# Attention's end in a four-layer graph network: one quad summed per stage of the last softmax, and the last scores ahead of the small TensorE steps

## The reference, cut to what matters

```python
q = x @ Wq + bq; k = x @ Wk + bk; v = x @ Wv + bv; skip = x @ Ws + bs
logits = jnp.sum(q[dst] * k[src], axis=-1) * (1.0 / jnp.sqrt(d))
m = segment_max(logits, dst); e = jnp.exp(logits - m[dst]); z = segment_sum(e, dst)
alpha = e / jnp.maximum(z[dst], 1e-16)
x = segment_sum(alpha[:, None] * v[src], dst) + skip       # relu after layers 1 and 2
```

## Time and profile before

| | us |
|---|---|
| three executions | 7211.72, 7203.6, 7215.84 |
| median | 7211.72 |
| span of the profiled execution | 7212.5 |
| ends of the three attention layers, from small step 0 of piece 13 to the last add | 41.29, 39.97, 37.98 |

### The profile page before, as it was taken

How to read it: one execution, slowest core, us unless ns; L and a number is a source line. 1 busy time by engine, 2 the same in 40 slices (tenths; PEclk the granted TensorE clock), 3 DMA queues, 4 the chain that set the end, 5 groups by cost and what they waited for, 6 DMA issues and landing times. The chain is left out here.

```text
span 7212.5 us, 119527 instructions
## 1 busy us (share of the span) xinstructions
PE 5515.6 (76%) x30306; PEld 4153.5 (58%) x30345; DVE 4706.7 (65%) x20339; ACT 2265.8 (31%) x5973; POOL 4972.2 (69%) x5179
## 2 busy tenths in 40 slices
PE   5675667776777766777777776789899997889887
PEld 4442344555666555566656665666666665667665
DVE  7985668466666446666636666664544546888887
ACT  1044442211114311113421111543333333554454
POOL 5777765677777477777577777647576574777774
PEclk6687888788888878888878888889999998988898
DMA  9433352577777467767557777657566773222222
GB/s 306 135 79 88 78 114 52 155 204 207 206 208 218 149 186 210 208 203 216 175 165 210 208 208 206 204 164 211 166 208 188 210 208 93 56 57 56 56 57 54
DMA packets 911842, 1151.30 MB, mean 160 GB/s; under 512 B 143281, under 2 KB 676465, under 8 KB 911249
## 3 DMA queue, kind: packets, MB, share of 16 engines
q1 hardware_dynamic: 689440, 673.54, 30.9%
q0 software_dynamic: 202464, 461.07, 23.9%
q10 hardware_dynamic: 19346, 9.66, 0.5%
HBM read 882.09 MB, written 261.74 MB: 159 GB/s over the span
## 5 line engine op out<-in xcount | busy, mean ns | idle before, releaser
L500 POOL DMA_INDIRECT G<-table_kv,idx x2496 | 2383.7, 955 | 966.5 <-issue 753.8
L1710 DVE SCALAR_TENSOR_TENSOR sums<-ramp,place,bank 128x128 f32<-128x128 f32 x2496 | 717.4, 342 | 1192.0 <-PE bank L1629 1098.4
L1619 PE MATMUL bank<-ident,G 128*128 128x128 f32 x2496 | 637.9, 334 | 720.1 <-DMA G<-table_kv,idx 713.5
L2144 POOL DMA_INDIRECT G<-table_h,src_idx x864 | 828.4, 959 | 465.0 <-issue 252.0
L1598 ACT COPY slab<-bank 128x512 f32<-128x512 f32 x624 | 364.8, 585 | 2295.3 <-PE bank L1619 2294.6
L500 POOL DMA_INDIRECT G<-table_h,idx x832 | 826.3, 993 | 298.2 <-issue 226.7
L1629 PE MATMUL bank<-qT,slab 128*128 x4992 | 915.5, 341 | 100.3 <-issue 80.4
L1629 PEld LDWEIGHTS bank<-qT,slab 128*128 128x128 f32 x4992 | 803.1, 244 | 196.0 <-issue 195.2
L1619 PEld LDWEIGHTS bank<-ident,G 128*128 128x128 f32 x2496 | 377.6, 163 | 931.2 <-DMA G<-table_kv,idx 891.7
L1841 DVE TENSOR_SCALAR OH<-ramp,place,weight 128x128 f32<-128x128 f32 x2076 | 715.4, 354 | 15.6 <-issue 8.5
L2128 PE MATMUL bank<-sums,qT 128*128 128x418 bf16 (+1 forms) x3528 | 676.4, 334 | 38.7 <-DVE same L2051 13.9
(11 more groups left out here) (355 smaller groups left out, 9538.6 us busy)
## 6 DMA issues: line engine op xcount, KB each, us to landing
stash<-G SPq DMA_DIRECT2D x312, 512.0 KB
sums<-stash SPq DMA_DIRECT2D x624, 256.0 KB
sums<-adjacency SPq DMA_DIRECT2D x294, 522.5 KB
adjacency<-same SPq DMA_DIRECT2D x49, 1184.0 KB, 13.9
same<-adjacency SPq DMA_DIRECT2D x90, 522.5 KB
G<-table_kv,idx POOLq DMA_INDIRECT x2496
sums<-adjacency SPq DMA_DIRECT2D x48, 408.0 KB
table_kv<-G SPq DMA_DIRECT2D x72, 256.0 KB, 3.2
```

The costliest lines, as they stand in the source:

```text
L500: pool.indirect_dma_start(G[:, s, 0:width], None, tab, bass.IndirectOffsetOnAxis(ap=idx[:, s:s + 1], axis=0)).then_inc(c_gather[s].sem, 16)
L1619: ins = pe.transpose(bank[q % 2][:, (s % QUAD) * P:(s % QUAD + 1) * P], G[:, s, 0:D], ident[:])
L1710: ins = dve.scalar_tensor_tensor(scratch[:, s, :], ramp[:], place[:, n * QUAD + s:n * QUAD + s + 1], bank[2 + q % 2][:, s * P:(s + 1) * P] ...
L2144: pool.indirect_dma_start(G[:, s, 0:D], None, table[l], bass.IndirectOffsetOnAxis(ap=src_idx[:, DENSE + t:DENSE + t + 1], axis=0)).then_in ...
```

## The change

```diff
@@ sums_by_slot
-                most = 1 if n < HASTE else 2
+                most = 1 if n < HASTE or ALL_QUADS <= n < weights_slot(PIECES - 1) else 2
                 found[n] = []
                 while len(found[n]) < most and q < ALL_QUADS and weights_slot(piece_of(q)) + (piece_of(q) >= HASTY_PIECE) <= n:
+                    if found[n] and q == LAST:
+                        break
                     found[n].append(q)
...
-        RESCALED = {c: weights_slot(c) if c >= HASTY_PIECE else SUM_SLOT[first_quad(c)] for c in range(PIECES)}
+        RESCALED = {c: max(weights_slot(c), SUM_SLOT[first_quad(c) - 1]) if c >= HASTY_PIECE else SUM_SLOT[first_quad(c)] for c in range(PIECES)}
+        FIRST_ONEHOTS = {c: max(weights_slot(c), SUM_SLOT[first_quad(c) - 2]) for c in range(HASTY_PIECE, PIECES)}
@@ first_onehots
-            return [first_quad(c) + k for c in (0, *range(HASTY_PIECE, PIECES)) if (weights_slot(c) if c else LAG_QUADS) == n for k in range(2)]
+            return [first_quad(c) + k for c in (0, *range(HASTY_PIECE, PIECES)) if (FIRST_ONEHOTS[c] if c else LAG_QUADS) == n for k in range(2)]
@@ act_attention
-                for x in first_onehots(n) + [onehot_ahead(x) for x in SUMS.get(n, ())]:
+                for x in [onehot_ahead(x) for x in SUMS.get(n, ())] + first_onehots(n):
@@ pe_attention
                 if n < ALL_QUADS:
                     turn(n)
+                if n == ALL_QUADS:
+                    scores(n - 1)
                 for c, k in stages_in(n - 2)[1:]:
                     if k in HOP_OF_STAGE:
                         hop(c, HOP_OF_STAGE[k])
-                if 0 < n <= ALL_QUADS:
+                if 0 < n < ALL_QUADS:
                     scores(n - 1)
```

More of the change, by code:

```diff
@@ L1485, in sums_by_slot @@
             return found
+        LAST = first_quad(PIECES - 1)
         SUMS = sums_by_slot()
@@ L1489, in build_program @@
         ALL_SLOTS = max(SUMS) + 1
-        RESCALED = {c: weights_slot(c) if c >= HASTY_PIECE else SUM_SLOT[first_quad(c)] for c in range(PIECES)}
+        RESCALED = {c: max(weights_slot(c), SUM_SLOT[first_quad(c) - 1]) if c >= HASTY_PIECE else SUM_SLOT[first_quad(c)] for c in range(PIECES)}
         DRAIN = min(q for q in range(ALL_QUADS) if SUM_SLOT[q] >= ALL_QUADS)
-        LAST = first_quad(PIECES - 1)
+        FIRST_ONEHOTS = {c: max(weights_slot(c), SUM_SLOT[first_quad(c) - 2]) for c in range(HASTY_PIECE, PIECES)}
         assert all(RESCALED[c] < SUM_SLOT[first_quad(c)] and SUM_SLOT[first_quad(c) - 1] <= RESCALED[c] for c in range(HASTY_PIECE, PIECES)) and LATE <= DRAIN <= LAST
```

## The result

The changed kernel took 7184.52 us (median of seven executions, 7176.61 to 7204.17) against 7211.72 us for the kernel before (seven, 7202.08 to 7215.84): a ratio of 0.9971, 95% interval 0.9962 to 0.9981, that is 13.7 to 27.4 us less; the two medians differ by 27.2. The forecast was 7188.6 us, 23.1 less.

The account below looks back on a forecast made before the run. Attention's body waits for gathered rows; only the three ends, waiting on small steps queued behind sums, can shorten. 27.5 won minus 3.0 (clock) minus 1.35 (scores) gives 23.1 us less: 7188.6 us median, range 7182 to 7201.

Parts of the forecast that it names:

- What bounds: At the three ends, 119.24 us in all, no engine is full; small steps wait behind two quads' sums, ScalarE for weights.
- The chain: Softmax steps of the third end, each behind one sum: L1757 2.3 us earlier, weights 11 to 12 us earlier than 4703.98.
- The ends: ScalarE runs at 1.59 us a quad, so each end takes 30.6 us; gains 10.7, 9.4 and 7.4, together 27.5.
- The allowance: Loss at the ends for TensorE sums at the low clock: 1.0 us a layer, 3.0 in all; bounds 0 and 11 a layer.
- The scores: Last scores moved ahead of step 4 of piece 12 make that step 0.45 us late, three times: 1.35 us lost.
- catches up: TensorE stands some 2 us for step 5, then recovers: a full-clock sum takes 1.18 us against ScalarE's 1.59 a quad.
- rival 1: At the ends TensorE's clock stays low half the time: only 12.9 us won, 7198.8 us; chance 0.12.
- rival 2: At the ends TensorE becomes the bound at 2.27 us a sum: 6.9 us lost, 7218.6 us; chance 0.05.
- rival 3: Something unseen keeps ScalarE's one-hots waiting after 196, or the next stage gives time back: 8 us won, 7204; chance 0.08.
- signs that I had named for being wrong: ScalarE's L1532 waiting for TensorE's sums or L1810, TensorE's L1675 waiting for a load, or ends shortening without the span.

Follow-up runs that it names:

- the sums alone: The changed kernel with the last scores put back behind small step 4 of piece 12; ratio to the kernel before 0.9983, ends 94.06 us in all.
- quad 198 ahead of step 5: The changed order of sums, last scores in their old place, with quad 198 joining 197 in slot 214; ratio to the kernel before 0.9972, ends 92.11 us.

## Why the prediction was right

**What bounds.** Right: small steps queued behind two sums held the softmax chain, and ScalarE stood for its weights. With one sum to a slot the weights came 12 us earlier against step 0 in the third end (14.5 and 13.2 in the others) and the wait was gone.

**The chain.** Worked out for the third end against measured, from step 0: L1757 4.5 and 4.6 us; L1772 8.9 and 9.2; weights 16.7 to 17.7 and 17.1; ScalarE's wait 2.2 and 2.46. ScalarE's last quad began 27.5 us after step 0 (26.9 worked out), at 4685.61; its pace of 1.59 held.

**The ends.** 30.6 plus 1.0 for the clock, 31.6 each, 94.8 in all; measured 94.28. The allowance came out partly by luck. I had 30.6 as 8.9 to L1772 and 21.7 from there to the last add; an end without slow sums took 21.87 for the second part. Of the 2.5 us by which the three ends lie above 3 x 30.6, the slow sums took 1.8 (0, 0.88 and 0.88) where I had 3.0, and the rest is the chain and ScalarE's path, each a little longer than worked out. Over the nine profiled ends of the changed kernel the clock fell around step 5 in seven, at 0.4 to 1.1 us each. The ends' old differences fit the clock too, but no run shows it by itself: in the kernel before, the third end had fewer sums at 1.2 GHz behind L1772 and took 25.6 us from there to the last add, the others 27.4 and 27.6; the first end was late at L1772 by another 1.5. What makes the clock fall in one end and not in another is open: in the first end of the changed kernel TensorE stood 2.13 us for step 5 at a clock that stayed at 1.00.
The Trainium skill (TensorE: Matmul & The Clock Gate, "What's actually happening") has the lower clock come after idleness. The second and third end agree (2.23 and 2.13 us of standing, then 0.63 over the next 4.6 us); the first, with the same stand, doesn't show it.

**The scores.** Right in sign, a third too small: 0.70 a layer, not 0.45.

**What the forecast had too simple.** It said that TensorE, after standing for step 5, "catches up" and that ScalarE alone sets the end. That holds only where the clock doesn't fall. Two paths have almost the same length: ScalarE's twelve quads behind the exponentials, 21.86 or 21.87 us from L1777 to the last add in all six such ends (of the changed kernel, the sums alone and quad 198 ahead of step 5), and the softmax chain with the adds locked into it and nine or ten sums behind. The second took 21.1 to 21.8 where the clock held and ScalarE had been shortened, and the stretch came to 22.3 to 23.1 where it fell. Lengthening ScalarE's path by 3.5 us gave 2.8 an end; shortening it by 1.6 gave about 0.35. I had priced TensorE against ScalarE's pace, but not the add of quad 197 behind stage 6.

**The rivals.** The clock didn't stay low (rival 1), TensorE didn't become slower than before (rival 2), nothing was given back in the ends (rival 3). But one of the signs that I had named for being wrong did show, in small: ScalarE's L1535 (L1532 before) waited 0.49 and 0.16 us for TensorE's sums in two of the three ends. It is rival 1 in small: 1.8 us for the slow sums in all, against its 13.2. The 12.9 us more behind the last end of the profiled execution stay a scatter of that execution: on another chip that stretch took 3031.5 us in the changed kernel and 3036.4 with the sums of before.

## What to carry to other kernels

When a chain of small steps on a shared, in-order engine feeds the last work, count what is queued ahead of each step; halving it was worth 6 to 10 us an end here, because the displaced sums found room behind the chain. Before shortening the engine that then looks full, look for a second path of nearly its length: read who releases that engine's slots, and what stands ahead of those instructions on their own engine. Where a gain is near the scatter of the times, measure the stretch itself: the three ends of the changed kernel add up to 94.28, 94.43 and 94.25 us on three chips whose totals differ by up to a third. But look at the clock in each: single ends differ by up to 1.1 us with it, and three of them don't resolve a gain of 0.35.

## What the runs showed of the hardware that was not expected

The kernel before took 7212 us on one chip and 9569 to 9664 on three others. The cause is open. The ends, in which only engines, their semaphores and small loads take part, were equal: for the changed kernel their sums differ by 0.2%. Between the first and the second end of the changed kernel there are 1105 us on the first chip, with 202 GB/s and a clock of 0.82, and 1537 on the second, with 145 GB/s and 0.70. From 250 to 1000 us, ahead of attention, DMA moved 77 GB/s on the first chip and 4 on the second. All profiled kernels on the other chips carry the assertion on SyncE and none of them ran on the first, so the runs don't part the chip from it; but the time is lost in attention's bodies too, where the assertion doesn't stand.

In the same program, TensorE's clock fell during or soon after the same stand of about 2.1 us in seven ends and stayed up in two. Where it fell, the sum of four products of 128 x 128 x 128 in fp32 behind it took up to 1.9 us instead of 1.05.
